# Four graph layers on one core: the comparison behind the transposed one-hot matrices reads the lane number from PSUM

## The reference

```python
def _gat_layer(h, W, al, ar, src, dst, residual):
    feat = (h @ W).reshape(N, H, D)
    el = jnp.sum(feat * al[None], axis=-1)
    er = jnp.sum(feat * ar[None], axis=-1)
    e = jax.nn.leaky_relu(el[src] + er[dst], NEG_SLOPE)
    m = jax.ops.segment_max(e, dst, num_segments=N)
    m = jnp.where(jnp.isfinite(m), m, jnp.zeros_like(m))
    ex = jnp.exp(e - m[dst])
    den = jax.ops.segment_sum(ex, dst, num_segments=N)
    a = ex / jnp.maximum(den[dst], jnp.asarray(1e-09, ex.dtype))
    out = jax.ops.segment_sum(a[:, :, None] * feat[src], dst, num_segments=N)
    if residual:
        out = out + h.reshape(N, H, D)
    return jax.nn.relu(out).reshape(N, H * D)
```

## Time and profile before

| | us |
|---|---|
| time, median of 3 runs | 6824.79 (6819.79 to 6827.75) |
| the profiled execution | 6842.32 |
| its span in the profile | 6840.5 |
| PE busy | 4942.9 (72%) |
| POOL busy | 4674.4 (68%) |
| DVE busy | 4237.9 (62%) |
| ACT busy | 2947.3 (43%) |

### The profile page before, as it was taken

One profiled execution on the slowest core, in us unless ns is written; L12 is line 12 of the kernel. 1 busy time (PEld: TensorE's weight loads), 2 busy tenths in 40 slices (PEclk: granted clock), 3 DMA queues, 4 the chain that ended last, 5 costly groups with the idle time before them and its releaser, 6 DMA issues. The chain is left out here.

```text
span 6840.5 us, 90191 instructions
## 1 busy us (share of the span) xinstructions
PE 4942.9 (72%) x16882; PEld 2919.8 (43%) x16882; DVE 4237.9 (62%) x11737; ACT 2947.3 (43%) x11807; POOL 4674.4 (68%) x4872
## 2 busy tenths in 40 slices
PE   9977777777777657777774777775677777677776
PEld 4445555544333334444442444443444444333333
DVE  5145555545555567777775777775777777555554
ACT  3310000000000057888885888785788888100000
POOL 0057777767777637777757777775777776677776
PEclk9988888877777777877786777776777777777777
DMA  6444444433333345455534555554454544333333
GB/s 203 157 132 118 119 118 118 118 97 105 105 105 105 97 139 140 138 141 139 140 109 123 142 138 143 139 142 132 136 138 136 141 137 118 99 111 112 111 112 103
DMA packets 409532, 864.73 MB, mean 126 GB/s; under 512 B 94925, under 2 KB 232678, under 8 KB 409002
## 3 DMA queue, kind: packets, MB, share of 16 engines
q0 software_dynamic: 233056, 642.19, 34.2%
q1 hardware_dynamic: 137040, 179.40, 8.2%
q10 hardware_dynamic: 38906, 37.37, 1.7%
HBM read 756.52 MB, written 102.07 MB: 126 GB/s over the span
## 5 line engine op out<-in xcount | busy, mean ns | idle before, releaser
L572 POOL DMA_INDIRECT rows_a<-table,rows_src x2496 | 2435.8, 976 | 958.4 <-issue 599.9
L712 PE MATMUL ps<-rows_a,hot_a 128*128 x4992 | 1967.0, 512 | 764.2 <-DMA rows_a<-table,rows_tile_a 328.9
L1812 ACT ACTIVATE rows_a<-rows_a,ex_a 128x64 f32<-128x64 f32 x9984 | 2415.7, 337 | 0.0
L1872 PE MATMUL ps<-rows_a,hot_a 128*128 128x260 f32 x4992 | 1908.8, 505 | 164.4 <-DVE agg L1730 144.8
L618 POOL DMA_INDIRECT rows_a<-table,rows_tile_a x1564 | 1484.3, 949 | 551.7 <-issue 256.7
L660 DVE TENSOR_TENSOR agg<-agg,ps 128x256 f32 (+1 forms) x2496 | 1048.5, 420 | 1303.2 <-PE ps L712 1265.2
L712 PEld LDWEIGHTS ps<-rows_a,hot_a 128*128 128x128 f32 x4992 | 1053.3, 242 | 1598.1 <-DVE agg L660 808.3
L1730 DVE TENSOR_TENSOR agg<-agg,ps 128x260 f32 x2496 | 1039.1, 416 | 341.9 <-PE ps L1872 199.9
L1872 PEld LDWEIGHTS ps<-rows_a,hot_a 128*128 128x128 f32 x4992 | 1032.6, 238 | 457.7 <-issue 326.7
L618 POOL DMA_INDIRECT rows_a<-table,row x782 | 743.7, 951 | 238.6 <-issue 131.8
L1957 ACT ACTIVATE root_a<-mv_a,eps 128x1 f32<-128x1 f32 x49 | 14.4, 295 | 978.6 <-DVE mv_a L1980 978.6
(11 more groups left out here) (328 smaller groups left out, 4090.8 us busy)
## 6 DMA issues: line engine op xcount, KB each, us to landing
dstt_a<-dloc_dram SPq DMA_DIRECT2D x156, 512.0 KB
table<-ob SPq DMA_DIRECT2D x49, 1024.0 KB, 4.4
rows_a<-table,rows_src POOLq DMA_INDIRECT x2496, 2.8
rows_a<-table,rows_tile_a POOLq DMA_INDIRECT x1564, 2.8
table<-ob_n SPq DMA_DIRECT2D x98, 130.0 KB, 2.7
rows_a<-table,row POOLq DMA_INDIRECT x782, 2.8
x_dram<-cur ACTq DMA_DIRECT2D x1, 6400.0 KB, 29.7
cur<-x_dram ACTq DMA_DIRECT2D x1, 6400.0 KB, 33.7
```

The source lines that it names most:

```text
L572: nc.gpsimd.indirect_dma_start(out=rows[:, n % ring, 0:width], out_offset=None, in_=table, in_offset=bass.IndirectOffsetOnAxis(ap=index[:, ...
L712: nc.tensor.matmul(ps[n % banks][:, 0:width], hot[:, m % nbuf, j, :], mine[n % 4], start=True, stop=True).then_inc(step_done, 1)
L1812: ins = nc.scalar.mul(a, a, ex[:, k % GV, s, h:h + 1])
L1872: nc.tensor.matmul(ps[j % banks][:, 0:W4], hot[:, j, :], rows[:, k % GV * UG + j, :], start=True, stop=True).then_inc(step_done, 1)
```

## The change

`hott` is made by a two-tensor comparison in place of a comparison with a scalar. Its second operand is one column of PSUM bank 7, beside `count`, which holds the partition number and is spread along the row of 2048. One copy a layer fills that column before the batches begin. All types, shapes, semaphores and buffers are otherwise those of before.

```diff
-        count = ps[7][:, 0:P]
+        count, lane = ps[7][:, 0:P], ps[7][:, P:P + 1]
...
                 nc.vector.tensor_copy(part(0), er_all[:]).then_inc(er_parts, 1)
+                nc.vector.tensor_copy(lane, iota_p[:])
                 nc.vector.tensor_copy(count, iota_f[:]).then_inc(counted, 1)
...
-                    nc.vector.tensor_scalar(hot_t[:], dst_t[:, k % 2, :], iota_p[:], None, ALU.is_equal).then_inc(hott_ready, 1)
+                    nc.vector.tensor_tensor(hot_t[:], dst_t[:, k % 2, :], lane.to_broadcast([P, UG * P]),
+                                            ALU.is_equal).then_inc(hott_ready, 1)
```

## The result

The changed kernel takes 6800.83 us (median of 7 runs, 6794.28 to 6803.86) against 6824.79; the ratio is 0.9965, its interval 0.9956 to 0.9974. That is 18 to 30 us less: faster by more than the 0.2% that count as no change. The time lies inside the range (6792 to 6852) and at the better edge of what rival A was given (6800 to 6810), not at the 6824 put down.

A forecast was written before the change was run, and what follows sets the result against it. POOL's issue of gathers was taken as the bound. Terms -19.7 + 0 + 17 + 0 + 4.3 = +1.6 us on 6842.3 gave 6844, as median 6826; 6824, no change, was put down, range 6792 to 6852.

The forecast's parts named there:

- rival A: Steady batches: moved VectorE instructions fall between gather starts, so the gain is kept; 6800 to 6810 us, chance 0.30.
- likeliest case: Whole kernel: no change, 6824 us put down, chance 0.44; alone it would span 6812 to 6838.
- The price of the comparison: VectorE, each batch: the new comparison takes 2273 ns against 793, +1.48 us a batch, 231 us in all.
- It is hidden in the steady part: Batch's end: VectorE's 2.46 us wait for rows absorbs the added 1.48, leaving 0.98; cost 0.
- The port is freed beside L1638: Gathers beside the old comparison: its port or lock against POOL goes, so their stretches vanish, -19.7 us at most.
- L1721 moves into POOL's way: Rescaling, moved back 1.43 us, covers a gather's start: 0.16 us in 123 batches, +19.7 at most, +17 taken.
- The other instructions: Other VectorE instructions with both inputs in SBUF shift against the gathers too: between -20 and +20 us, 0 taken.
- The ends of the layers: After each layer's last gather nothing hides the longer comparison: 1.43 us three times, +4.3 us.
- The starts of the layers: Layer starts: VectorE waits for first rows anyway, so the added column copy, some 0.15 us three times, costs 0.

The follow-up runs named there:

- the experiment with the longer comparison: The changed kernel with a second comparison of half the width behind the first in each batch: 6923.73 us, 1.0153 of the kernel before.
- The experiment with the later batches alone: The kernel before, with the new comparison in all batches of each attention layer but the first, which keeps the old one: 0.9994 of the kernel before.
- the first batch alone: The kernel before, with the new comparison only in the first batch of each attention layer, the old one in the other 51: 0.9968 of the kernel before.

## Why the prediction was right in its range and wrong in its likeliest case

- **The price of the comparison**, 2273 ns by extrapolation: 2279 measured. Right.
- **It is hidden in the steady part:** L1646's wait in the first middle fell from 2.46 us a batch to 37.6 us in 49 batches, 0.77; 0.98 was forecast. No pause of POOL between gathers is over 0.32 us in the three layers. Right, and the experiment with the longer comparison shows how near the edge it was.
- **The port is freed beside L1638, -19.7 us:** right: no gather is stretched by L1639. That is so for one input in PSUM; with both in SBUF, the same length costs +3.3%.
- **L1721 moves into POOL's way, +17 us:** 11.1 us in 61 gathers. The kind was right, the size too large, since the instruction's places against the gathers spread where the forecast let all 123 stay together.
- **The other instructions, 0:** 44.1 - 19.7 = 24.4 us before, 33.2 - 11.1 = 22.1 after. Near it. All stretches together went down by 10.9 us; the mean gather in the middles is 0.960, 0.954 and 0.963 us, of which 0.003 less is the pace, against 0.963, 0.962 and 0.973. The experiment with the later batches alone bears out that little of the gain comes from there.
- **The ends of the layers, +4.3 us:** +0.9 and +1.2 between layers, and from the last gather of the third layer to the first of the next stage 54.5 us before and 58.0 after, +3.6. In all +5.7: the right kind, a little short at the last.
- **The starts of the layers, 0:** this is the step that failed. The prediction said that "at a layer's start VectorE waits for the first rows anyway", and looked there for what the change costs, not for what the old form did. The three gathers of 8.2 to 9.4 us were in the trace, and in the mean of 976 ns in the earlier trace rows; the median in the earlier trace rows and the three even middles in the earlier trace rows leave them out. With -23 us the sum is -19.7 + 17 + 4.3 - 23 = -21, 6803 on the median's scale. The runs with the first batch alone and with one wait more show the term by itself: 0.9968 and 0.9969.

That the time fell inside the range is in part luck: rival A came out on the number and not on its reason. The gain that A counted on, of the later batches, is not to be told from nothing (0.9994); what made the number is the term at the layers' starts, which neither the likeliest case nor A had.

## What to carry to other kernels

Where GpSimd's issue of gathers is the bound, list every gather that is longer than the plain one, at the edges of a stage too, and set beside it not only what VectorE runs but what is queued next on it. A longer VectorE instruction with one input in PSUM can be worth more than a short one that holds the port, as long as the wait that hides it is measured first (2.46 us here for 1.49). Where the hold comes from waiting in line, one semaphore wait in front of the short instruction gives as much (0.9969). And freeing one of several such instructions may only make room for the next (0.9965 with one, 0.9923 with all).

## What the hardware showed that I had not expected

- The old comparison, ready behind a memset of 10.89 us, made a gather 7.2 to 8.5 us too long, all but some 0.6 us of that while only the memset ran; with one wait that kept it from being handed over, nothing was held. The same stands in the later batches on a smaller scale: 18 of 20 gathers that began during an addition with an instruction of two SBUF inputs next in line were 0.34 to 0.53 us too long, and none of 33 once one of its inputs lay in PSUM.
- A gather under way when the blocking instruction ended was stretched by the overlap less 0.12 to 0.14 us, for 0.2 to 1.6 us of overlap, with the old comparison (0.79 us) and with the long one that has both inputs in SBUF (2.28 us).
- POOL's plain gather takes 949 ns in some executions and 946 in others, in changed and unchanged stages alike; over 4842 gathers that moves a profiled span by some 15 us, more than half of what this change is worth.
